# A macaron transformer block on one core: new order tables for the first, middle and last batches

## The reference, cut to what matters

```python
x = x + 0.5 * ffn(layernorm(x))      # "a"
x = x + attn(layernorm(x))           # "att"
x = x + 0.5 * ffn(layernorm(x))      # "c"
# x: (8, 512, 128).  attn: 16 heads of 64; q, k RMS-normalized; causal;
#   bias[i, j] = -(i - j) * softplus(omega) * slope * softplus(k_j . u / 8)
#   y = softmax(q k^T / 8 + bias) v;  return y @ Wproj
# ffn: hidden 512, gelu; both weights get a small term made of 16 tokens of x
```

## Time and profile before

| | |
|---|---|
| median of 3 runs | 756.89 us (756.16 to 758.61) |
| profiled execution | 755.66 us, of which span 753.9 us |
| PE, DVE busy | 728.3 us (97%), 653.3 us (87%) |
| ACT, POOL busy | 641.6 us (85%), 646.7 us (86%) |
| granted TensorE clock | 1.00 over the whole span |
| DMA queue q1 | 58.19 MB, 35.6% of 16 engines |
| chain that ended last | PE 74%, ACT 13%, DVE 8%, issue 3%, POOL 2% |

### The profile page before, as it was taken

One profiled execution on the slowest core, in us unless ns is written; L12 is line 12 of the kernel. 1 busy time (PEld: TensorE's weight loads), 2 busy tenths in 40 slices (PEclk: granted clock), 3 DMA queues, 4 the chain that ended last, 5 costly groups with the idle time before them and its releaser, 6 DMA issues.

```text
span 753.9 us, 25070 instructions
## 1 busy us (share of the span) xinstructions
PE 728.3 (97%) x9273; PEld 522.6 (69%) x9273; DVE 653.3 (87%) x2126; ACT 641.6 (85%) x1424; POOL 646.7 (86%) x760
## 2 busy tenths in 40 slices
PE   6789999999999999999999999999999999999987
PEld 4347667677767776687667777677776876678765
DVE  7889789988888898987989879888889879899976
ACT  8878798888988799888998889987998879986673
POOL 6738889898998989989998999989899899998690
PEclk9999999999999999999999999999999999999999
DMA  6232315251345406334254433344043441434421
GB/s 174 42 97 77 73 36 138 58 114 33 75 98 100 101 3 120 82 87 87 44 94 73 98 68 72 87 99 106 13 105 84 99 87 29 103 72 109 93 44 29
DMA packets 99617, 60.32 MB, mean 80 GB/s; under 512 B 74622, under 2 KB 86400, under 8 KB 99496
## 3 DMA queue, kind: packets, MB, share of 16 engines
q1 hardware_dynamic: 99336, 58.19, 35.6%
q10 hardware_dynamic: 160, 0.52, 0.3%
HBM read 4.74 MB, written 2.10 MB: 9 GB/s over the span
## 4 chain that ended last, share of the span: by engine, by line
PE 74%; ACT 13%; DVE 8%; issue 3%; POOL 2%; DMA 0%; DVEq 0%; ACTq 0%; POOLq 0%
PE ps L1123 13%; PE ps L1125 13%; PE ps L1124 13%; PE ps L1254 8%; PE ps L1280 8%; PE ps L1281 8%; PE ps L1236 4%; ACT qk L1059 3%; PE ps L1282 3%; ACT pt L1084 2%; DVE maxima L1609 2%; ACT hid L996 2%; PE ps L1140 1%; ACT L996 1%; ACT sq L1006 1%
## 5 line engine op out<-in xcount | busy, mean ns | idle before, releaser
L852 POOL TENSOR_TENSOR pt_l<-pt 128x512 f16<-128x512 f32 x366 | 321.4, 907 | 36.2 <-ACT pt L1084 34.5
L1605 DVE CUSTOM_DVE_ANT_0 masked<-ps,causal_row 128x512 f16<-128x512 f32 x480 | 205.7, 486 | 27.4 <-PE ps L1254 26.5
L1084 ACT ACTIVATE pt<-ps 128x512 f32<-128x512 f32 (+1 forms) x384 | 174.6, 534 | 16.3 <-PE ps L1282 15.5
L1280 PE MATMUL ps<-qk 128*128 128x512 f16 (+3 forms) x512 | 146.7, 300 | 0.0
L1281 PE MATMUL ps<-qk 128*128 128x512 f16 (+3 forms) x512 | 146.5, 299 | 0.0
L878 POOL TENSOR_TENSOR qkn<-qkn,rs 128x512 f32<-128x512 f32 x128 | 130.8, 1050 | 13.5 <-ACT rs L1018 12.9
L1123 PE MATMUL ps<-v_buf,pt 128*128 128x65 f16 x1280 | 129.8, 194 | 2.7 <-DVE ytok L1620 1.6
L1124 PE MATMUL ps<-v_buf,pt 128*128 128x65 f16 x1280 | 129.8, 194 | 0.0
L1125 PE MATMUL ps<-v_buf,pt_l 128*128 128x65 f16 x1280 | 129.6, 194 | 0.0
L1123 PEld LDWEIGHTS ps<-v_buf,pt 128*128 128x128 bf16 x1280 | 118.0, 98 | 8.0 <-issue 4.5
L1124 PEld LDWEIGHTS ps<-v_buf,pt 128*128 128x128 bf16 x1280 | 117.5, 98 | 1.7
(11 more groups left out here) (213 smaller groups left out, 1935.4 us busy)
## 6 DMA issues: line engine op xcount, KB each, us to landing
qk<-qk SPq DMA_DIRECT2D x128, 128.0 KB, 2.4
qk<-qk SPq DMA_DIRECT2D x62, 256.0 KB, 3.7
x_in<-in_L_attn_x SPq DMA_DIRECT2D x8, 256.0 KB, 3.1
out<-x_out SPq DMA_DIRECT2D x7, 256.0 KB, 2.3
qk<-qk SPq DMA_DIRECT2D x1, 1024.0 KB, 7.4
qk<-gtt SPq DMA_DIRECT2D x64, 8.0 KB
qk<-nmt SPq DMA_DIRECT2D x64, 2.0 KB
y_hl<-ytt SPq DMA_TRANSPOSE x62, 3.1
```

What stands on the lines that cost most here:

```text
L852: g.tensor_tensor(pt_l[:, h % 2, c], pt[:, h % 2, c], pt_h[:, h % 2, c], ALU.subtract).then_inc(s_pt_l, 1)
L1084: a.activation(pt[:, h % 2, c], ps[:, j, 0:width], ACT.Exp).then_inc(s_exp, 1)
L1280: pe.matmul(dst, k1(h)[:, keys], q1(h)[:, kb * P:T], start=True, stop=False)
L1605: ins = d.tensor_tensor_reduce(masked[:, part.unit(s, i)[0], col:col + (ib + 1) * P], part.bank(s, i)[:, col:col + (ib + 1) * P], causal_r ...
```

## The change

Only `ORDER` is changed. In `first`, `body` and `final` of all five engines the same entries stand in another order. `lead` and `tail` are unchanged, and so are all stage functions; no instruction is added or dropped. The table is one line longer, so every line number behind it is one higher than before (L852 becomes L853). Cut to the entries that are spoken of (each hunk has more lines like these):

```diff
 "tensor" "first":
-            ("s", 7, THIS), ("a", 12, THIS), ("v", 1, 3, THIS), ("pv", 6, THIS), ("zt", "att", NEXT), ("s", 8, THIS),
+            ("pv", 5, THIS), ("a", 12, THIS), ("v", 1, 3, THIS), ("pv", 6, THIS), ("zt", "att", NEXT), ("s", 8, THIS),
...
 "tensor" "body":
-            ("pv", 1, THIS), ("s", 3, THIS), ("m", "a", NEXT), ("pv", 2, THIS), ("a", 8, THIS), ("s", 4, THIS),
-            ("pv", 3, THIS), ("v", 1, 3, THIS), ("s", 5, THIS), ("a", 9, THIS), ("h", "a", NEXT), ("s", 6, THIS),
-            ("a", 10, THIS), ("wp", 0, THIS), ("pv", 4, THIS), ("a", 11, THIS), ("out", "a", NEXT), ("nm", 2, THIS),
+            ("pv", 1, THIS), ("s", 3, THIS), ("m", "a", NEXT), ("s", 4, THIS), ("pv", 2, THIS), ("a", 8, THIS),
+            ("v", 1, 3, THIS), ("pv", 3, THIS), ("a", 9, THIS), ("s", 5, THIS), ("h", "a", NEXT), ("s", 6, THIS),
+            ("a", 10, THIS), ("pv", 4, THIS), ("a", 11, THIS), ("wp", 0, THIS), ("out", "a", NEXT), ("nm", 2, THIS),
...
```

More of the change, by code:

```diff
@@ new lines @@
+            ("ln2", "a", NEXT), ("s", 4, THIS), ("zt", "a", NEXT), ("yt", 1, THIS), ("s", 5, THIS), ("m", "a", NEXT),
+            ("h", "a", NEXT), ("s", 6, THIS), ("v", 1, 2, THIS), ("nm", 2, THIS), ("ln1", "att", NEXT),
+            ("ln2", "att", NEXT), ("v", 1, 3, THIS), ("s", 7, THIS), ("zt", "att", NEXT), ("yt", 2, THIS),
+            ("s", 8, THIS), ("qk", 0, 0, NEXT), ("qk", 0, 1, NEXT), ("qk", 0, 2, NEXT), ("qkn", 0, 0, NEXT),
+            ("v", 0, 0, NEXT), ("qk", 0, 3, NEXT), ("qk", 1, 0, NEXT), ("s", 9, THIS), ("yt", 3, THIS),
@@ L125 @@
+            ("qkn", 2, 1, NEXT), ("qk", 3, 1, NEXT), ("s", 14, THIS), ("qk", 3, 2, NEXT), ("qk", 3, 3, NEXT),
+            ("qkn", 3, 0, NEXT), ("nm", 0, NEXT), ("qkn", 3, 1, NEXT), ("yt", 6, THIS), ("t", 4, NEXT),
+            ("s", 15, THIS), ("gate", 1, NEXT), ("t", 5, NEXT), ("t", 6, NEXT), ("nm", 1, NEXT),
         ],
@@ L202 @@
-            ("wp", 2, THIS), ("pv", 14, THIS), ("t", 5, NEXT), ("t", 6, NEXT),
+            ("pv", 0, THIS), ("gr", 1, THIS), ("v", 1, 1, THIS), ("v", 1, 2, THIS), ("wp", 3, LAST), ("pv", 1, THIS),
+            ("zt", "a", NEXT), ("m", "a", NEXT), ("pv", 2, THIS), ("a", 8, THIS), ("pv", 3, THIS), ("v", 1, 3, THIS),
+            ("a", 9, THIS), ("ln1", "c", LAST), ("a", 10, THIS), ("a", 11, THIS), ("ln2", "c", LAST), ("pv", 4, THIS),
+            ("wp", 0, THIS), ("add", "a", NEXT), ("ln1", "att", NEXT), ("pv", 5, THIS), ("zt", "c", LAST),
@@ L265 @@
-            ("yt", 6, THIS),
+            ("ln1", "a", NEXT), ("rows", 2, THIS), ("gd", 2, THIS), ("gd", 3, THIS), ("rows", 3, THIS),
+            ("swap", 2, THIS), ("yt", 0, THIS), ("back", 2, THIS), ("yt", 1, THIS), ("swap", 3, THIS),
+            ("nm", 2, THIS), ("yt", 2, THIS), ("yt", 3, THIS), ("back", 3, THIS), ("nm", 3, THIS), ("rows", 0, NEXT),
+            ("gd", 0, NEXT), ("gd", 1, NEXT), ("yt", 4, THIS), ("swap", 0, NEXT), ("rows", 1, NEXT), ("yt", 5, THIS),
+            ("swap", 1, NEXT), ("back", 0, NEXT), ("back", 1, NEXT), ("nm", 0, NEXT), ("yt", 6, THIS),
@@ L273 @@
-            ("back", 1, NEXT), ("nm", 1, NEXT), ("yt", 6, THIS),
+            ("ln1", "a", NEXT), ("yt", 7, LAST), ("rows", 2, THIS), ("gd", 2, THIS), ("rows", 3, THIS),
+            ("swap", 2, THIS), ("swap", 3, THIS), ("gd", 3, THIS), ("yt", 0, THIS), ("yt", 1, THIS),
+            ("back", 2, THIS), ("nm", 2, THIS), ("yt", 2, THIS), ("yt", 3, THIS), ("nm", 3, THIS), ("back", 3, THIS),
+            ("rows", 0, NEXT), ("gd", 0, NEXT), ("swap", 0, NEXT), ("gd", 1, NEXT), ("rows", 1, NEXT),
+            ("yt", 4, THIS), ("yt", 5, THIS), ("back", 0, NEXT), ("swap", 1, NEXT), ("add", "c", LAST),
```

200 lines of the change are left out of this document (91 added, 109 removed).

## The result

The change made the kernel slower: 759.08 us in the median of 22 runs (757.55 to 762.06), against 756.48 (755.17 to 758.61) for the kernel before, run on the same chips. The ratio is 1.0031, with a 95% interval of 1.0021 to 1.0040, so some 2.4 us. I had forecast 756.4. The profiled execution took 757.57 us (span 755.8), 1.9 more than the profiled one before. All ratios in this document are of fast executions; two that ran far longer, 3756 us of `first_only` and 2613 us of `end_only`, are not in them.

The account below looks back on a forecast made before the run. PE was taken to bound the kernel, leaving about 3.2 us of pauses per middle batch. Terms -0.6 + 0.95 + 0.25 - 1.1 = -0.5 us gave 755.2 profiled, 756.4 us as median; range 752.8 to 759.2.

Parts of the forecast that it names:

- Last batch, end: End of last batch: `pv 14` goes ahead of `h c` and `pv 15` starts earlier, -1.1 us (bounds 0, -2.0).
- I take the 3.13 measured, since POOL was busy beside it then too: End of last batch: VectorE's `pl 15`, moved earlier, still takes 3.13 us, so ends at 730.1 and `pv 15` starts at 731.4.
- The price that I had worked out beside this rule: End of last batch: if `pl 15`'s three each wait for a whole POOL instruction, no gain; sum 1.1 us higher.
- My check of it: End of last batch: `pl 15`'s three at up to 1.67 us are 5.0 us, putting `pv 15` at 732.6, no gain.
- Last batch, start: Start of last batch: `pv 7` gains 0.1, `nm 3` loses 0.35 as DVE idles some 0.6 us for `v 1 0`: +0.25 us.
- First batch: First batch: late `s 7` delays POOL's `pl 7`, second `qkn` of quarter 1 and `t 2`: +0.95 us (bounds 0, +2.1).
- the step on `t 2`: First batch: `t 2` needs the second `qkn`, ending at 117.7, so loses 0.8 us, of which PE makes up 0.3.
- Middle batches: Six middle batches: pauses before `pv 3` and `pv 7` go, less a loss at `m a`; 0.1 a batch, -0.6 us.
- the 0.26 inside `h c`: Middle batches: bank for `h c` freed earlier, worth 0.26, counted as nothing since the first `a` behind waits more.
- Rival A: Middle batches: DVE's lag not taken up, each 0.37 us longer instead of 0.1 shorter; +2.8, so 759.2; chance 0.17.
- rival B: Middle batches: `h c`'s 0.26 and the 0.29 behind it go, 0.7 us gained each; -3.6, so 752.8; chance 0.20.
- Rival C: Middle batches: room for DMAs does nothing; late y transposes before `wp 3` return by chance, 0.8 us up or down; no chance given.

Follow-up runs that it names:

- first_only: The kernel before with the change's new order of the first batch alone: 757.38 us, 1.0018 to the kernel before.
- end_only: The kernel before with three last-batch moves (`pv 14` ahead of `h c`, `s 15` of `yt 6`, `pl 14` of `m c`): 756.39 us, 0.9995.
- end_hold: `end_only` with GpSimd's last-batch `yt 6` waiting for `pl 15` and the second half of `m c` behind `yt 6`: 754.11 us, 0.9972 to the kernel before.
- after_hold: The whole change with GpSimd's last-batch `yt 6` waiting for `pl 15` and the second half of `m c` behind it: 756.79 us, 1.0008 to the kernel before.
- final_pl0: `final_only` with VectorE's `pl 0` put back ahead of `v 1 0`: 757.20 us, 1.0006 to the kernel before.
- final_pv1: `final_only` with VectorE's `pv 1` put back ahead of `pl 2`: 756.65 us, 0.9999 to the kernel before.
- s7_only: The kernel before with one move, ScalarE's `s 7` ahead of `yt 2` in the last batch: 756.54 us, 1.0004.
- final_only: The kernel before with the change's new order of the last batch alone: 756.78 us, 1.0004 to the kernel before.

## Why the prediction was wrong, point by point

The sum was -0.5 us and the traces show +1.9. The end of the last batch makes 1.1 of the difference, the middle batches 1.0, the start of the last batch 0.4.

**Last batch, end: -1.1 forecast, 0.0 found.** The step that failed is "I take the 3.13 measured, since POOL was busy beside it then too". I took `pl 15`'s length to be its own, when it was made by where GpSimd's instructions ended. `pl 15` is three subtractions with both inputs in SBUF, 1.75 us in `end_hold` beside an almost quiet GpSimd. In the kernel before, 1.4 of its 3.13 us were already waiting inside them, to the end of an instruction of GpSimd's each time. Moving `pl 15` earlier changed only which ones. `end_only` shows the term at zero, `end_hold` and `after_hold` show 1.4 us of gain once GpSimd stands still. The Trainium skill's rule (SBUF — State Buffer, "SBUF: two separate sides") is that such a VectorE instruction and one of GpSimd's hold the shared port as an exclusive lock. The traces agree: 0.68 us alone became 1.64 beside GpSimd, ending 0.55 behind it. The price that I had worked out beside this rule, no gain at the end, was right. I had set it beside the sum and should have put it in. (My check of it, three times 1.67 us, counted the third subtraction, of 256 columns and 0.41 us alone, as if it had 512.)

**Last batch, start: +0.25 forecast, +0.68 found.** I costed VectorE's 0.6 us of idle time, paid in part. The idle time was there, but taking 0.4 of it away changed nothing (`final_pl0`). The loss is again `pl 2` standing through an instruction of GpSimd's, and `pv 1` behind it (`final_pv1`, 0.55 of the 0.68). The gain before `pv 7` was none at all, even in the kernel before (`s7_only`).

**First batch: +0.95 forecast, +0.95 found, by luck.** The chain that I summed was not the one that cost. ScalarE's `s 7` ended at 95.9 and POOL's `pl 7` at 97.9 (forecast 96.3 and 98.3). But the second `qkn` of quarter 1 ended at 116.8, not 117.7, and `t 2` started at 116.9 where I had it 0.8 late. So the step on `t 2` failed. Left out was that the batch hands 0.4 us on to the next, through the DMA for `x_in` that is now issued behind `nm 1` (read from the traces; no run moved it alone): `first_only` costs 1.4 us.

**Middle batches: -0.6 forecast, +0.4 found.** Quiet ones are 0.02 to 0.12 shorter, near the 0.1 forecast, by other terms. Won were `pv 3`'s 0.14 and the 0.26 inside `h c`, which I had put at nothing since the first `a` behind it would wait more; it waits 0.29 as before. Of `pv 7`'s 0.16 nothing was won (it and `zt att` now wait 0.23 together, `pv 7` 0.21 before). `wp 0` cost 0.2 where I counted nothing, `a 2` 0.05 as forecast, and `t 1` and `wp 1` 0.15. `m a` lost nothing where I had 0.12, since `z_hl` takes 0.28 when it starts at the very end of one of GpSimd's instructions (0.11 before it), in place of 0.63 with 0.49 of one still to go. The 0.6 us of loss in the first three are the lateness handed on (`m a` held 0.36 in the first), and a late landing in the third that was not there before (0.35 before `wp 3`). I had put both at nothing. My working also has a slip: its matmuls add up to 85.8 us and not 85.5, so that PE stands for 2.9 us of a middle batch and the bound is 17 us; nothing else rests on it.

**The rivals.** Rival A's time, 759.2, is next to the 759.08 measured, but its mechanism is not what happened: a quiet middle batch was to be 0.37 longer and is no longer than before. Of rival B one half came true, the 0.26 inside `h c`, and the other did not (the first `a` behind it waits 0.29 as before), and no middle batch gained the 0.7. Rival C said that late landings come back by chance. In the second and third middle batch they don't: they come with instruction loads at about the same place in every trace of an order. Before the first middle batch a load did move, by 2.5 us between two kernels alike up to there, and `x_in` was later still with it, in four of eight traces.

**The median.** The traces differ by 1.9 us, the medians by 2.6. Part of it can be the late `x_in`: at a granted clock of 1.00 over the span the changed kernel took 757.57 to 759.03 us (8 executions), the kernel before 754.87 to 756.16 (37), and the changed kernel's trace is one of the early ones. That its slower executions at this clock are the late ones is likely but not shown. In other executions TensorE's granted clock falls to the 1.2 GHz level for 3.4 us, in a few traces for 6.8, here or there. Busy time in windows, `final_only`, then the kernel before, then `end_hold`:

```profile
735.00:740.00 5.00, 5.00 (x54) 4.82 (x55) 1.97 (x4) 0.60 (x1) 1.34 (x2) 0.66 0.00 0
```

```profile
735.00:740.00 5.00, 4.81 (x84) 4.55 (x82) 3.43 (x12) 0.90 (x2) 0.70 (x1) 1.00 0.02 5
```

```profile
735.00:740.00 5.00, 4.89 (x72) 4.18 (x70) 3.89 (x17) 1.79 (x3) 0.45 (x1) 1.00 0.02 5
```

The row at 0.66 follows the waits of `pv 14`, `pv 15` and `yx`, and `wp 2` takes 1.2 us longer there. It comes in some executions and not in others of a kernel with the same waits. The profiled executions of both kernels had none of it. `end_hold` has shorter waits there, and its 12 runs lie within 2.0 us (753.49 to 755.44) where those of the kernel before, 29 beside it, lie within 3.9. Of its 12, 9 ran at a granted clock of 0.999 or more over the span, of the 29 only 8. Those alone differ by 1.3 us in the median (753.88 against 755.14), near the 1.4 that the trace shows at the end. So the rest of the 2.1 us is the clock that falls less often. (Its profiled execution is 2.2 us shorter than that of the kernel before, but 0.6 of this is a second middle batch of 88.96 in place of 89.54, where the transpose landed after 4.1 us and not 4.6.)

## What to carry to other kernels

A duration in a trace may hold another engine's: before a VectorE instruction with two SBUF inputs is costed by its row, look at what GpSimd does beside it, and where the row ends. If it ends a fixed time behind one of GpSimd's, moving it earlier buys nothing; here a wait that kept GpSimd off for 1.6 us bought 1.4 us, more than any order tried. A pause on the busiest engine is worth what the other engines behind it allow. Putting back one stage of a new order told little in the first batch (none of five gave anything back), because the other streams were written for it. The sync engine's issues are part of the order too: look at what each one now stands behind.
